# First feed-forward of a graph network kernel: tile results stored to one DRAM row per token and choice, summed at the end

## The reference, cut to what matters

```
logits = flat @ router_w.T                     # 625 x 8 experts
top_w, top_i = lax.top_k(softmax(logits), 2)   # each token chooses 2 of 8 experts
top_w = top_w / top_w.sum(-1, keepdims=True)
for e in range(8):
    w_e = sum(top_w * (top_i == e))            # 0 for a token that did not choose e
    h = gelu(flat @ w1[e] + b1[e])             # 768 -> 192
    out = out + w_e * (h @ w2[e] + b2[e])      # 192 -> 768
x = x + out
```

## Time and profile before

| | us |
|---|---|
| three runs | 1595.2, 1598.59, 1599.29 (median 1598.59) |
| the profiled execution | 1595.69, of which 1593.7 are the span of the trace |
| TensorE / VectorE / ScalarE / GpSimd busy over the span | 1243.8 / 885.8 / 726.3 / 705.0 |
| first feed-forward, barrier to barrier | about 502 to 714 |
| its accumulating stores, first start to last start | 580.87 to 700.05 |
| second feed-forward | 1420 to 1593.7 |

### The profile page before, as it was taken

One profiled execution on the slowest core, in us unless ns is written; L12 is line 12 of the kernel. 1 busy time (PEld: TensorE's weight loads), 2 busy tenths in 40 slices (PEclk: granted clock), 3 DMA queues, 4 the chain that ended last, 5 costly groups with the idle time before them and its releaser, 6 DMA issues. The chain is left out here.

```text
span 1593.7 us, 32659 instructions
## 1 busy us (share of the span) xinstructions
PE 1243.8 (78%) x9846; PEld 935.2 (59%) x9847; DVE 885.8 (56%) x1703; ACT 726.3 (46%) x1089; POOL 705.0 (44%) x816
## 2 busy tenths in 40 slices
PE   8998565973774367836589999999999994873996
PEld 6776454873642355625456666666666663643774
DVE  8952677876664543336266656656666555765000
ACT  8994302864142253424144555545655533220653
POOL 0076736776575513320245555555555550010243
PEclk9999675895876579877799999999999996985998
DMA  1000200002133577648388999989999985725352
GB/s 58 1 1 4 80 17 1 1 1 80 34 96 76 170 246 205 214 113 327 117 233 246 276 291 266 268 257 277 293 285 274 281 231 158 245 65 184 81 108 51
DMA packets 116422, 247.40 MB, mean 155 GB/s; under 512 B 25354, under 2 KB 53511, under 8 KB 116220
## 3 DMA queue, kind: packets, MB, share of 16 engines
q1 hardware_dynamic: 80668, 162.88, 30.1%
q0 software_dynamic: 35680, 83.54, 23.5%
HBM read 215.14 MB, written 60.28 MB: 173 GB/s over the span
## 5 line engine op out<-in xcount | busy, mean ns | idle before, releaser
L646 PE MATMUL r_pO<-ring,r_rowsT 128*128 x2520 | 422.4, 327 | 0.0
L646 PEld LDWEIGHTS r_pO<-ring,r_rowsT 128*128 128x128 f16 x2520 | 244.3, 98 | 154.8 <-issue 1.6
L1861 DVE SCALAR_TENSOR_TENSOR ring<-q_wstage,ring 128x768 f16<-128x768 f32 x198 | 175.1, 952 | 57.8 <-ACT ring L1820 55.7
L1801 POOL DMA_INDIRECT acc_dram<-r_msg,r_scol x70 | 126.5, 1807 | 165.5 <-PE r_pT L1922 123.9
L1820 ACT ACTIVATE ring<-q_wstage 128x768 f16<-128x768 f32 x198 | 148.8, 829 | 26.1 <-issue 26.1
L479 POOL DMA_INDIRECT inv_col<-qinv_dram,pair_col x112 | 124.1, 1108 | 77.1 <-POOL pair_col L492 70.6
L1849 ACT ACTIVATE r_msg<-r_pO,slot_inv 128x768 f32<-128x768 f32 x70 | 62.9, 898 | 192.7 <-PE r_pO L646 192.4
L429 POOL DMA_INDIRECT slot_dram<-table_record,table_rowi x80 | 101.7, 1271 | 104.0 <-issue 103.4
L392 PE MATMUL acc<-oh_d,oh_s 125*125 125x512 f16 (+1 forms) x800 | 136.7, 310 | 0.0
L1922 PE MATMUL r_pT<-r_S,q_parts 128*128 128x128 f16 x852 | 101.6, 222 | 10.3 <-DVE r_S L1878 7.3
L1868 DVE TENSOR_TENSOR r_rowsT<-r_pT,r_rowsT 128x512 f16<-128x512 f32 x71 | 48.7, 686 | 101.9 <-ACT r_rowsT L1829 101.8
(11 more groups left out here) (402 smaller groups left out, 2493.0 us busy)
## 6 DMA issues: line engine op xcount, KB each, us to landing
q_wstage<-in_L_gnn_W_rel_dram SPq DMA_DIRECT2D x33, 2304.0 KB, 14.6
stage<-in_L_gnn_W_dram SPq DMA_DIRECT2D x6, 768.0 KB, 5.8
wparts<-in_L_ffn_w_dram SPq DMA_DIRECT2D x8, 576.0 KB, 5.9
f_stage<-in_L_ffn_w_dram SPq DMA_DIRECT2D x8, 576.0 KB, 11.5
f_stage<-in_L_ffn_w_fast_dram SPq DMA_DIRECT2D x8, 576.0 KB, 7.3
f_stage<-in_L_ffn_w_slow_dram SPq DMA_DIRECT2D x8, 576.0 KB, 8.5
f_stage<-in_L_ffn_h_fast_dram SPq DMA_DIRECT2D x8, 576.0 KB, 10.2
down_dram<-f_stage SPq DMA_DIRECT2D x8, 576.0 KB, 3.8
```

Source lines behind the costliest of these rows:

```text
L646: ins = eng.matmul(out, x, w[:, h * n:(h + 1) * n], start=first and x is xh and w is wh, stop=last and x is xl, **kw)
L1801: eng.indirect_dma_start(out=K.acc_dram[u % 2], out_offset=bass.IndirectOffsetOnAxis(ap=scol[:, u:u + 1], axis=0), in_=msg[:, u, :], in_of ...
L1861: ins_ = eng.scalar_tensor_tensor(wring[:, slot, 1, k, :], wstage[:, slot, k, :], W_SCALE, wring[:, slot, 0, k, :], ALU.mult, ALU.subtract)
```

## The change

The results of layer 0 are no longer accumulated in DRAM. `y_dram` gets 2N = 1250 rows, one for each token and choice, and each tile's store is a plain indirect write. Nothing orders these stores among each other; each waits for its `y` only, and a `y` buffer is free when the store that used it has landed (one semaphore for each of the 5 buffers). The seed is left out for layer 0. `row` now runs to 1250, and `token` is found from it by two more small instructions on VectorE. At the end SyncE loads both rows of each token (into `sums`, which lies where the up weights were), GpSimd adds the two, and VectorE adds the sum to `K.x` and takes the statistics. Layer 1 stays as it was.

```diff
+        second = sb("second", [128, FTILES], FP32)
+        s_wrote = [K.sem("f%d_wrote%d" % (layer, u)) for u in range(YS)]
+        if layer == 0:
+            sums = K.up[:, :, :, :, :].rearrange("q a k e f -> q (a k e f)")[0:P, 0:4 * NT * C].bitcast(FP32).rearrange("p (i a c) -> p i a c", i=NT, a=2)
@@ SyncE, before the loop
-            eng.dma_start(acc.rearrange("(i p) c -> p i c", p=P), K.x[:, :, :]).then_inc(s["seeded"], 16)
+            if layer == 1:
+                eng.dma_start(K.out.rearrange("(i p) c -> p i c", p=P), K.x[:, :, :]).then_inc(s["seeded"], 16)
@@ SyncE, at the end
-            eng.wait_ge(s["scattered"], 16 * FTILES)
             if layer == 0:
+                for u in range(YS):
+                    eng.wait_ge(s_wrote[u], 16 * len(range(u, FTILES, YS)))
+                eng.wait_ge(s["up_ready"], FTILES)
+                both = K.y_dram.rearrange("(a n) c -> n a c", a=2)
                 for i in range(NT):
                     for p, q in ((0, 112), (112, P)):
-                        eng.dma_start(K.x[p:q, i, :], acc[i * P + p:i * P + q, :]).then_inc(summed[i], 16)
+                        eng.dma_start(sums[p:q, i, :, :], both[i * P + p:i * P + q, :, :]).then_inc(summed[i], 16)
@@ GpSimd
             def scatter(t):
                 eng.wait_ge(s["y_ready"], t + 1)
+                if layer == 0:
+                    eng.indirect_dma_start(out=K.y_dram, out_offset=bass.IndirectOffsetOnAxis(ap=row[:, t:t + 1], axis=0),
+                                           in_=y[:, t % YS, :], in_offset=None, bounds_check=2 * N - 1, oob_is_err=False
+                                           ).then_inc(s_wrote[t % YS], 16)
+                    return
@@ GpSimd, behind the loop
-            eng.wait_ge(s["scattered"], 16 * FTILES)
+            if layer == 0:
+                for i in range(NT):
+                    eng.wait_ge(summed[i], 32)
+                    eng.tensor_tensor(sums[:, i, 0, :], sums[:, i, 0, :], sums[:, i, 1, :], ALU.add).then_inc(s["choices_added"], 1)
@@ VectorE, tables
-            eng.tensor_scalar(token[:, :], table[:, 0, :], -1.0, 0.0, ALU.add, ALU.max).then_inc(s["tokens_ready"], 1)
+            if layer == 0:
+                link(eng.tensor_scalar(second[:, :], table[:, 0, :], N + 1.0, -float(N), ALU.is_ge, ALU.mult))
+                link(eng.scalar_tensor_tensor(second[:, :], table[:, 0, :], -1.0, second[:, :], ALU.add, ALU.add))
+                eng.tensor_scalar(token[:, :], second[:, :], 0.0, None, ALU.max).then_inc(s["tokens_ready"], 1)
@@ VectorE, at the end
                 for i in range(NT):
-                    eng.wait_ge(summed[i], 32)
+                    eng.wait_ge(s["choices_added"], i + 1)
+                    eng.tensor_tensor(K.x[:, i, :], K.x[:, i, :], sums[:, i, 0, :], ALU.add).then_inc(s["x_added"], 1)
+                    eng.wait_ge(s["x_added"], i + 1)
                     measure(K, eng, i)
@@ ScalarE, weigh(t)
-                if t >= YS:
+                if t >= YS and layer == 0:
+                    eng.wait_ge(s_wrote[t % YS], 16 * (t // YS))
+                elif t >= YS:
                     eng.wait_ge(s["scattered"], 16 * (t - YS + 1))
```

More of the change, by code:

```diff
@@ L1171, in ffn_phase @@
             "b2_ready", "b2_placed", "stored", "seeded", "down_loaded", "cut_hi", "cut_lo", "set_merged", "set_cut", "set_stored", "turned", "evicted", "up_ready", "relu_ready", "h_ready", "h_hi", "h_lo",
-            "down_ready", "y_ready", "scattered", "pair_ready") + tuple("gathered_%d" % b for b in range(IDX_BUFS))}
+            "down_ready", "y_ready", "scattered", "choices_added", "x_added", "pair_ready") + tuple("gathered_%d" % b for b in range(IDX_BUFS))}
         s_down = [K.sem("f%d_down_chunk%d" % (layer, c)) for c in range(DOWNS)]
@@ L1176, in ffn_phase @@
         summed = [K.sem("f%d_summed%d" % (layer, i)) for i in range(NT)]
-        acc = K.y_dram if layer == 0 else K.out
+        s_wrote = [K.sem("f%d_wrote%d" % (layer, u)) for u in range(YS)]
+        if layer == 0:
+            sums = K.up[:, :, :, :, :].rearrange("q a k e f -> q (a k e f)")[0:P, 0:4 * NT * C].bitcast(FP32).rearrange("p (i a c) -> p i a c", i=NT, a=2)
         pX = psum[:, 0:2, :].bitcast(FP16).rearrange("p b n -> p (b n)")[:, 0:2 * C]
@@ L1232, in _ @@
             eng.wait_ge(s["stored"], 16)
-            eng.wait_ge(s["scattered"], 16 * FTILES)
             if layer == 0:
+                for u in range(YS):
+                    eng.wait_ge(s_wrote[u], 16 * len(range(u, FTILES, YS)))
+                eng.wait_ge(s["up_ready"], FTILES)
+                both = K.y_dram.rearrange("(a n) c -> n a c", a=2)
                 for i in range(NT):
                     for p, q in ((0, 112), (112, P)):
-                        eng.dma_start(K.x[p:q, i, :], acc[i * P + p:i * P + q, :]).then_inc(summed[i], 16)
+                        eng.dma_start(sums[p:q, i, :, :], both[i * P + p:i * P + q, :, :]).then_inc(summed[i], 16)
+            else:
+                eng.wait_ge(s["scattered"], 16 * FTILES)
         @block.gpsimd
@@ L1271, in scatter @@
                     eng.wait_ge(s["scattered"], 16 * t)
-                eng.indirect_dma_start(out=acc, out_offset=bass.IndirectOffsetOnAxis(ap=row[:, t:t + 1], axis=0),
+                eng.indirect_dma_start(out=K.out, out_offset=bass.IndirectOffsetOnAxis(ap=row[:, t:t + 1], axis=0),
                                        in_=y[:, t % YS, :], in_offset=None, bounds_check=N - 1, oob_is_err=False, compute_op=ALU.add
@@ L1398, in _ @@
             table = psum[:, 6, 0:3 * FTILES].rearrange("p (v t) -> p v t", v=3)
-            eng.tensor_scalar(token[:, :], table[:, 0, :], -1.0, 0.0, ALU.add, ALU.max).then_inc(s["tokens_ready"], 1)
-            link(eng.tensor_scalar(empty[:, :], table[:, 0, :], 0.0, 2.0 * N, ALU.is_equal, ALU.mult))
+            if layer == 0:
+                link(eng.tensor_scalar(second[:, :], table[:, 0, :], N + 1.0, -float(N), ALU.is_ge, ALU.mult))
+                link(eng.scalar_tensor_tensor(second[:, :], table[:, 0, :], -1.0, second[:, :], ALU.add, ALU.add))
+                eng.tensor_scalar(token[:, :], second[:, :], 0.0, None, ALU.max).then_inc(s["tokens_ready"], 1)
+            else:
+                eng.tensor_scalar(token[:, :], table[:, 0, :], -1.0, 0.0, ALU.add, ALU.max).then_inc(s["tokens_ready"], 1)
+            link(eng.tensor_scalar(empty[:, :], table[:, 0, :], 0.0, 4.0 * N, ALU.is_equal, ALU.mult))
             eng.scalar_tensor_tensor(row[:, :], table[:, 0, :], -1.0, empty[:, :], ALU.add, ALU.add).then_inc(s["rows_ready"], 1)
@@ L2154, in build @@
         K.xn_dram = nc.dram_tensor("xn_dram", (N, 2 * C), FP16).ap()
-        K.y_dram = nc.dram_tensor("y_dram", (N, C), FP32).ap()
+        K.y_dram = nc.dram_tensor("y_dram", (2 * N, C), FP32).ap()
         K.down_dram = nc.dram_tensor("down_dram", (EXP, 2, F * C), FP16).ap()
```

2 lines of the change are left out of this document (1 added, 1 removed).

## The result

| | before | after |
|---|---|---|
| four runs each, median (lowest to highest) | 1597.55 us (1595.2 to 1599.29) | 1575.42 us (1575.22 to 1581.57) |
| profiled execution, its span | 1595.69, 1593.7 | 1575.59, 1573.6 |

The ratio is 0.9875, 95% interval 0.9849 to 0.9901: faster by 1.25%, 1.0 to 1.5%. The prediction was 1570 (1554 to 1588), with the likeliest case A at 1560 to 1580.

What follows compares the result with a forecast made beforehand. GpSimd's waits for the store before were taken as the bound, with a two-tile dependence loop behind. Gains of 36.2 us (9.7 from the start) less 9.3 at the end gave -26.9, 1568.8; forecast 1570, range 1554 to 1588.

Steps and rivals of the forecast that it cites:

- case A: Tile loop: the store's order goes and the two-tile loop is what is left; 1560 to 1580 us, chance 0.60.
- Start: Before the tile loop: without the seed, small stores and down-weight cuts end sooner, first transposes follow; gain 9.7 us.
- my bound of 6.9: Before the loop: lower bound of the gain, 6.9 us, if VectorE's cuts hold the first gather too.
- L: Tile loop: time from a gather's start to its tile's transposes on TensorE; taken as 6.7 us, mean before 7.5.
- Loop: First store to tile 13's store: waits for the store before go, six double tiles at 12.7 us after the second store.
- 6.0 + L: Tile loop: least time for two tiles, from store issue, gather, transposes, copy, weighing and GpSimd's start; 12.7 us.
- Drain: From tile 13's store to the issue of the final loads, gathers being over: 14.1 us.
- Sums: Phase end: doubled loads, GpSimd's addition, VectorE's addition and statistics take 19.4 us instead of 10.1; loss 9.3 us.
- The rest costs nothing: Whole phase: `token` counted already, `y` buffer waits look five tiles back, down weights load earlier; no further cost.
- C: Rival in the tile loop: DMA keeps the pace, two tiles take 14.8 us; 1581 us, chance 0.18.
- B: Rival in the tile loop: TensorE becomes the bound at 5.2 us a tile; 1549 us, chance 0.12.
- D and E: Rivals: first, start's gain absent, slow gathers, 1591 us, chance 0.03; second, slower, DMAs pile up behind weight loads, chance 0.07.

Runs made afterwards that it cites:

- experiments 1 and 2: First: changed kernel with the seed kept ahead of the small stores, 1606.10 us. Second: kernel before with only the seed moved behind down-weight loads, 1588.43 us.
- Experiment 7: Changed kernel with VectorE's last four cuts waiting until GpSimd has issued the first four gathers; 1568.72 us.
- experiment 5: Changed kernel with every gather of the first feed-forward one place earlier, five ahead of the loop instead of four; 1564.89 us.
- Experiment 4: Changed kernel loading only the first two of the eight weight sets, merges still run all eight times; 1567.78 us.
- experiment 6: Changed kernel with both additions at the end on VectorE and none on GpSimd; 1573.71 us.
- experiment 3: Changed kernel with the order of the stores put back, each plain store waiting until the one before has landed; 1592.47 us.
- kernels 8 and 9: 8: changed kernel plus five gathers ahead, both additions on VectorE, first gathers before VectorE's cuts, 1556.53 us; 9: the same with merges one tile later, 1565.09 us.

## Why the prediction was right, step by step

The sum was -26.9 us and the phase shows -17.8; the time came out at 1575.4, 5.4 above the forecast and inside both ranges. That it is so near has luck in it: the phase missed its sum by 9.1 us, and 2.3 us came back from phases that were not changed. Sign and main mechanism were right, and the terms as follows.

**Start: -9.7 predicted, -9.6 measured; so close a match is luck, since two steps were off.** The seed as the cause is shown by experiments 1 and 2. The small stores ended at 533.3 (said: near 531). One of the gathers stands at 550.15 (said: 549.6), but it did not wait for the end of VectorE's cuts, at 550.66: it began 0.30 us behind the gather before it, whose issue had taken 2.33 us beside the cuts. Experiment 7 shows that the cuts were what delayed both. Nor did the first one slip in ahead, at 542.3: GpSimd was still at its last copies, which the cuts stretched to 3.36 us, and started it at 547.51. That was my bound of 6.9. It cost less than that bound, since the second tile's transposes did not have to queue behind the first tile's copy: they waited 4.03 us more for their rows. They stand 54.3 us into the phase, where 556.3 - 502.7 = 53.6 was said. From the gather at 550.15 to these transposes L was 8.2 and not 6.7; the gather's earlier place in the phase (46.2 us into it, 46.9 said) made up for half of that. The first copy of a tile came at 554.31 and not near 550.

**Loop: 81.4 us predicted, 86.6 measured; this term was mis-sized by 5.2.** That a latency in the loop of two tiles was the bound is what experiment 5 shows: one gather more of lead, and the loop runs at TensorE's pace. The failed step is "I take L = 6.7". L is not one number here: one gather in four comes late. The one at 573.90 is issued right behind a burst of three weight loads (571.24 to 572.75) and its transposes stand at 582.91, L = 9.0, with TensorE idle for 3.29 us ahead of them. Two more such waits follow, at 609.66 (L = 8.5) and 636.96 (L = 9.0), each behind a burst. There the chain of the forecast holds step by step: 1.02 for the issue (1.7 taken), 0.30, L, 1.46 for the transposes (0.84 taken), copy, weighing and 0.80 make 5.9 + L, and the store of tile 2 stands 14.9 us behind that of tile 0. The two tiles that follow each time take 12.4 us, and there the chain is not what ends last: their transposes, at 595.89 for one, wait for no gather but for TensorE's own work. From the second store on, twelve tiles take 81.2 us (659.12 - 577.89), 13.5 for two where 12.7 was said. By the formula of 6.0 + L this would be L = 7.5, the mean of before, but only because the two kinds of double tile average to it. (That mean was put down to nine tiles; the trace has eight transposes that wait for a gather there, with a mean of 7.7.) Experiment 4 confirms the weight loads as the cause of the late gathers.

The sum also had no term for TensorE's clock. These are the stretches from the late transposes to the next ones, and from those to the ones behind:

```profile
582.91:590.44 7.53, 7.23 (x61) 6.18 (x61) 0.55 (x2) 3.28 (x5) 1.99 (x2) 0.63 0.96 370
590.44:595.89 5.45, 5.45 (x61) 4.48 (x60) 3.26 (x4) 3.28 (x5) 1.22 (x2) 1.00 0.31 87
```

Behind its wait of 3.29 us TensorE was granted 0.63 of full speed, much of the stretch at the lower of its two levels, and one tile's work took 7.53 us instead of 5.45. It is the same behind the two other waits, with 7.75 and 7.57 us. So a late gather costs twice: the three waits are 9.8 us, and the 778 matmuls of the loop kept TensorE busy for 76.20 us against 69.84 in experiment 5, 6.4 more. Together that is 16.2 of the 16.5 us between the two loops. What I had written of the clock ahead, 1.00 in most of the tile loop, hides this: over the loop it was 0.88, before and after the earlier trace rows, and 1.00 only where no gather came late.

My argument that a gather no longer stands behind a store that reads and writes had something in it: in the loop, the twelve gathers landed 7.7 us behind their issue in the median before and 4.6 after. It does not help the gathers behind a weight burst, and those set the pace.

**Drain: -3.9 predicted, -4.7 measured.** Right.

**Sums: +9.3 predicted, +12.1 measured.** 2.8 too little, from three small errors: the first addition starts 6.16 us behind the first issue (4.85 taken), the tiles follow each other in 3.05 us (2.74 taken; (690.80 - 678.61) / 4), and the addition takes 1.80 (1.5 taken). The rows of the load from two arrays were near, but somewhat fast for this. For the addition, the Trainium skill's table ("GPSIMD Engine Reference", section 3.1) had led to an estimate of 1.7; the trace says 1.80.

**Exit: 0 predicted, +1.8 measured.** "The rest costs nothing" missed it. With GpSimd's last addition only 5.0 us ahead of the next phase, the barrier opens later; experiment 6 takes that back.

**The rivals.** A is what happened: 1575 lies in its own range, at the slow side. C (DMA keeps the pace) is refuted by experiment 5, though its observation was right: the long L stands beside weight loads. The price of contention here is latency on single gathers, and the clock that falls behind it, and not throughput, so it can be bought off by lead. B (TensorE becomes the bound) happened for half of the double tiles, at a clock partly low, and as a whole only in experiments 4 and 5, at 72.0 and 70.1 us for thirteen tiles. D and E did not occur.

**What stays open:** how the 10.8 us of experiment 3 divide between the issue and the DMA engines' time; and why the second graph layer, untouched, takes between 704 and 718 us from run to run.

## What to carry to other kernels

When a wait is removed, write down the next loop of dependences with all its terms, take the latency in it from the rows in which the engine really waited (here 8.5 to 9.5 us behind a burst of loads, where 6.7 was taken), add what TensorE's lower clock costs behind each wait, and ask whether the issue can simply stand one step earlier: here one more gather ahead of the loop was worth 15 us, nearly as much as the whole change, and the best version (kernels 8 and 9) is 2.4 to 2.5% faster than before against 1.25% for the change alone. A big DMA that nobody waits for still costs what stands behind it in its queue: moving it took a line or two and made the phase 7.3 us shorter. Before a busy DMA share is named as the bound, look at whether latency or throughput is what runs out: the share rose from 0.75 to 0.89 when the order of issue allowed it.

## What the hardware showed that I had not expected

- An indirect store that accumulates takes GpSimd 1.59 us to issue, a plain one 1.02. From issue to landing the median of the 17 stores is 6.1 us before, 5.8 with plain stores in order and 4.7 without order. The packets of GpSimd's queue for the same 8.14 MB took the 16 DMA engines 36.8 us with accumulating stores and 22.6 with plain ones in order (24.5 in the changed kernel, 28.3% of 86.6).
- TensorE's granted clock was 0.63 over the 7.5 us behind a wait of 3.3 us, and one tile's 61 matmuls took 7.5 instead of 5.4 us; in the loops without such waits it was 1.00.
- VectorE's instructions with two inputs in SBUF stretch not only GpSimd's copies (3.36 us for two, against 0.18 each) but also the issue of a gather (2.33 against 0.97). Beside VectorE's merges in the loop, gathers took 0.97 to 2.08 us.
- From the last statistics through the barrier took 3.0 us and not 1.1 where GpSimd's last addition had ended only 2.1 us before the statistics did (692.60, 694.65).
- While the sums were loaded, the DMA engines stood at a share of 1.04 at 257 GB/s; in experiment 5's loop they moved 317 GB/s at a share of only 0.89. So the share does not stand for one figure of GB/s; it depends on the kind of transfer.
